# Attention kernel on one core: two buffers for the summed exponentials, narrower columns of maxima, and a rearranged set-up

## The reference, cut to what matters

```python
x = x + proj(softmax(q k^T / sqrt(128)) v)            # q, k, v from group_norm(x): layer 0, one head
t = tokens(x)                                         # 1024 x 128
n = layer_norm(t)
sq, sk = n @ wq_s, n @ wk_s                           # 8 search heads of 16
retrieved = softmax(sq sk^T / 4) @ (n @ wv_r)         # 2 retrievers of 16
gate = softmax over the 2 retrievers of (n @ wq_r) . (retrieved @ wk_ret)
t = t + (gate * retrieved summed over retrievers) @ w_out
w_lora = NF4_TABLE[qidx].reshape(-1, 16) * scales[:, None]   # 128 x 128 codes of 4 bits
t = t + (layer_norm(t) @ w_lora^T) @ W^T
```

## Time and profile before

| what | us |
|---|---|
| median of 3 runs | 5034.42 (5031.06 to 5035.82) |
| the profiled execution | 5030.68 |
| its span | 5028.7 |
| PE busy in it | 4704.0 (94%) |
| POOL busy | 4250.0 (85%) |
| DVE busy | 3893.6 (77%) |
| ACT busy | 3302.2 (66%) |

### The profile page before, as it was taken

How to read it: one execution, slowest core, us unless ns; L and a number is a source line. 1 busy time by engine, 2 the same in 40 slices (tenths; PEclk the granted TensorE clock), 3 DMA queues, 4 the chain that set the end, 5 groups by cost and what they waited for, 6 DMA issues and landing times.

```text
span 5028.7 us, 102045 instructions
## 1 busy us (share of the span) xinstructions
PE 4704.0 (94%) x29838; PEld 2548.5 (51%) x29838; DVE 3893.6 (77%) x8176; ACT 3302.2 (66%) x6657; POOL 4250.0 (85%) x1173
## 2 busy tenths in 40 slices
PE   4899999999999999999999999999999999999986
PEld 3455555555555555555555455555455555555532
DVE  3688887888878888887778887878887878877763
ACT  2466766666766666766676766666767666766654
POOL 1388888888888988888988888988888988888887
PEclk9899999999999999999999999999999999999987
DMA  0111011111011111011111111111111111111010
GB/s 15 38 43 43 31 47 31 39 47 47 26 47 30 39 47 47 30 43 31 39 47 47 34 39 33 37 47 47 38 36 37 32 47 47 43 30 42 28 39 13
DMA packets 92739, 191.77 MB, mean 38 GB/s; under 512 B 16744, under 2 KB 50920, under 8 KB 92400
## 3 DMA queue, kind: packets, MB, share of 16 engines
q1 hardware_dynamic: 92400, 186.45, 12.8%
HBM read 17.53 MB, written 16.78 MB: 7 GB/s over the span
## 4 chain that ended last, share of the span: by engine, by line
issue 38%; PE 34%; POOL 17%; ACT 5%; DVE 5%; POOLq 0%; DMA 0%; ACTq 0%; DVEq 0%; SPq 0%
POOL p_sum L639 16%; PE ps_u L798 7%; PE ps_bank L785 5%; PE ps_bank L749 4%; PE ps_bank L673 4%; PE ps_bank L763 4%; ACT p L956 3%; DVE max_part L1061 2%; PE ps_bank L704 2%; PE ps_bank L807 2%; PE ps_bank L693 1%; PE ps_bank L684 1%; PE ps_bank L815 1%; PE ps_bank L735 1%; ACT h L884 1%
## 5 line engine op out<-in xcount | busy, mean ns | idle before, releaser
L639 POOL TENSOR_TENSOR p_sum<-p_sum,p 128x2048 f32<-128x2048 f32 x768 | 3505.5, 4564 | 266.9 <-ACT p L956 208.5
L1061 DVE TENSOR_REDUCE max_part<-ps_bank 128x1 f32<-128x512 f32 x4096 | 2551.8, 682 | 697.6 <-PE ps_bank L763 693.3
L956 ACT ACTIVATE p<-ps_bank 128x512 f32<-128x512 f32 x4096 | 2154.2, 606 | 704.2 <-PE ps_bank L785 690.9
L798 PE MATMUL ps_u<-p,rv 128*32 128x512 f32 x8192 | 1003.3, 608 | 2.7 <-ACT p L956 2.7
L785 PE MATMUL ps_bank<-q_stack,k_stack 64*128 64x512 f32 x4096 | 888.2, 461 | 105.9 <-ACT p L956 65.8
L639 POOL TENSOR_TENSOR p_sum<-p 128x2048 f32<-128x2048 f32 x128 | 584.1, 4563 | 375.4 <-ACT den_sb L967 205.0
L763 PE MATMUL ps_bank<-k_stack,q_stack 63*128 63x512 f32 x4096 | 828.8, 451 | 55.3 <-ACT p L956 21.7
L785 PEld LDWEIGHTS ps_bank<-q_stack,k_stack 64*128 64x128 f32 x4096 | 370.6, 185 | 665.4 <-ACT p L956 253.9
L763 PEld LDWEIGHTS ps_bank<-k_stack,q_stack 63*128 63x128 f32 x4096 | 363.4, 185 | 523.4 <-ACT p L956 160.5
L749 PE MATMUL ps_bank<-v,p 128*128 128x129 f32 x4096 | 508.6, 279 | 8.2 <-ACT p L956 6.7
L749 PEld LDWEIGHTS ps_bank<-v,p 128*128 128x128 f32 x4096 | 473.2, 191 | 61.1 <-ACT p L956 27.3
(11 more groups left out here) (140 smaller groups left out, 4438.6 us busy)
## 6 DMA issues: line engine op xcount, KB each, us to landing
k_stack<-k_hi SPq DMA_DIRECT2D x256, 128.0 KB, 2.6
q_stack<-q_hi SPq DMA_DIRECT2D x256, 128.0 KB, 2.8
x_sb<-in_x SPq DMA_DIRECT2D x32, 512.0 KB, 3.5
k_stack<-k_lo SPq DMA_DIRECT2D x128, 128.0 KB, 2.6
q_stack<-q_lo SPq DMA_DIRECT2D x128, 128.0 KB, 2.8
t_held<-t_front SPq DMA_DIRECT2D x32, 512.0 KB, 2.9
rqk<-tok_next SPq DMA_DIRECT2D x32, 512.0 KB, 3.6
t_core<-t_held SPq DMA_DIRECT2D x32, 512.0 KB, 3.0
```

Of the source, the lines that this page charges most:

```text
L639: pool.tensor_tensor(p_sum[:, :, :], before, p1[:, step % ring, :, :], ALU.add)\
L798: last = pe.matmul(ps_u[n * QUAD:(n + 1) * QUAD, :], rv[:, key_tile, :], p1[:, step % ring, n, :], start=(key_tile == 0), stop=(key_tile = ...
L956: act.activation(p1[:, step % ring, n, :], bank_of("scores", index // 2, n % 2), ACT.Exp, scale=scale1)\
L1061: dve.tensor_reduce(max_part1[:, phase % 2, i, n, half:half + 1], bank_of("max1", index // 2, side), AXIS.X, ALU.max)\
```

## The change

Four things change; the orders of the engines in the loop stay as they are.

1. `p_sum` gets two buffers, used in turn by phase. The first addition of a phase no longer waits for ACT's copy of the denominators of the phase before, but for TensorE's `den` of the phase before that one (`filled["den"]`), which read the same buffer.
2. The columns of maxima become narrow: `max_cols0` has 8 + 128 columns in place of 1024, `max_cols1` 16 + 128 in place of 512. The tiles that TensorE transposes now overlap; rows of the transposes beyond those used hold other maxima in place of zeros.
3. The 4-bit weight is decoded by DVE: a conversion, 15 independent comparisons into 15 tiles (the code whose value is zero is left out), one reduction over them and one multiplication with the scales. The codes and scales are the first two loads and have a semaphore of their own. The clearing of `k_stack`, `q_stack` and `max_row0` goes to POOL.
4. SP issues the `wk_ret` loads ahead of the rows of ones, and the first image's `x` is loaded between them, in the set-up; `load` returns at once for image 0.

```diff
-        p_sum = sb("p_sum", [P, GROUP, HALF])
+        p_sum = sb("p_sum", [P, 2, GROUP, HALF])
...
-        max_cols0 = sb("max_cols0", [P, tiles, P])
+        max_cols0 = sb("max_cols0", [P, tiles + P])
...
-        max_cols1 = sb("max_cols1", [P, tiles_per_half, P])
+        max_cols1 = sb("max_cols1", [P, tiles_per_half * GROUP + P])
...
+                sp.dma_start(q_index, qidx).then_inc(codes_loaded, 16)
+                sp.dma_start(block_scale[:, :], scales.rearrange("(o k) -> o k", o=P)).then_inc(codes_loaded, 16)
                 loads = [
...
+                sp.wait_ge(blocks_zeroed, 1)
+                for h in range(HEADS):
+                    rows = slice(h * HEAD_DIM, (h + 1) * HEAD_DIM)
+                    sp.dma_start(wk_ret_blocks[rows, rows], wk_ret).then_inc(weights_loaded, 16)
+                sp.dma_start(x_sb[:, :], x_dram[0:1, :, :].rearrange("b c n -> (b c) n")).then_inc(x_loaded, 16)
                 sp.wait_ge(stacks_cleared, 1)
                 for pair in range(PAIRS):
                     sp.dma_start(k_stack[ROWS - 1:2 * ROWS:ROWS, pair, :].bitcast(F32), out_sb[0:2, :])\
                       .then_inc(ones_rows_ready, 16)
...
-                pool.wait_ge(weights_loaded, 16 * (14 + HEADS))
-                link(pool.tensor_copy(q_value, q_index))
-                link(pool.memset(lora, 0.0))
-                for n, value in enumerate(NF4):
-                    link(pool.tensor_scalar(lora_part, q_value, float(n), float(value),
-                                            ALU.is_equal, ALU.mult))
-                    link(pool.tensor_tensor(lora, lora, lora_part, ALU.add))
...
+                pool.memset(out_sb[0:2, :], 1.0)
+                pool.memset(k_stack[:, :, :].bitcast(F32), 0.0).then_inc(stacks_cleared, 1)
+                pool.memset(q_stack[:, :, :].bitcast(F32), 0.0)
+                pool.memset(max_row0[:, :].bitcast(F32), 0.0)
...
+                dve.memset(max_cols0[:, :], 0.0)
+                dve.memset(max_cols1[:, :], 0.0)
+                dve.wait_ge(codes_loaded, 16 * 2)
+                link(dve.tensor_copy(q_value, q_index))
+                levels = [(float(n), value) for n, value in enumerate(NF4) if value]
+                for n, (code, value) in enumerate(levels):
+                    last = dve.tensor_scalar(decoded[:, n, :], q_value, code, value, ALU.is_equal, ALU.mult)
+                link(last)
+                link(dve.tensor_reduce(lora, decoded.rearrange("p n c -> p c n"), AXIS.X, ALU.add))
...
                     if key_tile == 1:
-                        wait(pool, den_evicted, phases * b + phase)
+                        wait(pool, filled["den"], phases * b + phase - 1)
...
-                    before = p1[:, (step - 1) % ring, :, :] if key_tile == 1 else p_sum[:, :, :]
-                    pool.tensor_tensor(p_sum[:, :, :], before, p1[:, step % ring, :, :], ALU.add)\
+                    before = p1[:, (step - 1) % ring, :, :] if key_tile == 1 else p_sum[:, phase % 2, :, :]
+                    pool.tensor_tensor(p_sum[:, phase % 2, :, :], before, p1[:, step % ring, :, :], ALU.add)\
```

More of the change, by code:

```diff
@@ L287, in build @@
         proj_rows, ffn_rows, wq_r_sb, wk_ret_blocks = (setup_tiles[:, n, :] for n in range(3, 7))
-        bias_v, proj_bias, q_value, lora, lora_part = (setup_tiles[:, n, :] for n in range(7, 12))
+        bias_v, proj_bias, q_value, lora = (setup_tiles[:, n, :] for n in range(7, 11))
         q_index = setup_tiles[:, 12, :].bitcast(I32)
         turned = setup_tiles[:, 13:17, :]
+        decoded = setup_tiles[:, 17:17 + len(NF4) - 1, :]
         qk_w = sb("qk_w", [P, 2, P])
@@ L363, in build @@
         weights_loaded = sem("weights_loaded")
+        codes_loaded = sem("codes_loaded")
+        x_loaded = sem("x_loaded")
         blocks_zeroed = sem("blocks_zeroed")
@@ L371, in build @@
         weights_ready = sem("weights_ready")
+        codes_decoded = sem("codes_decoded")
         stacks_cleared = sem("stacks_cleared")
@@ L382, in _ @@
                     (wq_sb[:, :], wq_s), (wk_sb[:, :], wk_s), (wv_r_sb[:, :], wv_r),
-                    (w_out_sb[:, :], w_out), (q_index, qidx),
-                    (block_scale[:, :], scales.rearrange("(o k) -> o k", o=P)),
+                    (w_out_sb[:, :], w_out),
                     (norm_cols[:, 0:1], norm_w.rearrange("(c a) -> c a", a=1)),
@@ L397, in _ @@
                       .then_inc(ones_rows_ready, 16)
[L398 to L401, removed]
             @block.gpsimd
@@ L469, in link @@
                     dve.wait_ge(links.sem, links.next())
[L471 to L476, removed]
+                dve.memset(max_cols0[:, :], 0.0)
[7 more added lines that the diff above has]
+                link(dve.tensor_reduce(lora, decoded.rearrange("p n c -> p c n"), AXIS.X, ALU.add))
+                dve.tensor_tensor(lora.rearrange("p (k j) -> p k j", j=NF4_BLOCK),
+                                  lora.rearrange("p (k j) -> p k j", j=NF4_BLOCK),
+                                  block_scale[:, :].unsqueeze(2).broadcast_to([P, P // NF4_BLOCK, NF4_BLOCK]),
+                                  ALU.mult).then_inc(codes_decoded, 1)
                 dve.wait_ge(pool_ready, 1)
                 dve.tensor_copy(first_row[:, :], ident[:, 0:1].broadcast_to([P, P]))
-                dve.wait_ge(weights_loaded, 16 * (14 + HEADS))
-                dve.tensor_scalar(bias_v, ones[:, :], qkv_bias[:, 2:3], None, ALU.mult)
+                dve.wait_ge(weights_loaded, 16 * (12 + HEADS))
+                dve.tensor_scalar(bias_v, ones[:, 0:1].broadcast_to([P, P]), qkv_bias[:, 2:3], None, ALU.mult)
                 dve.tensor_copy(token_w[:, P:P + HEAD_DIM], wv_r_sb[:, HEAD_DIM:])
@@ L557, in load @@
                 def load(b, index):
+                    if isinstance(b, int) and b == 0:
+                        return
                     wait(sp, h_ready, number_of(b))
@@ L722, in max_rows0 @@
                         last = pe.transpose(out[:, i * P:(i + 1) * P],
-                                            max_cols0[:, half * tiles_per_half + i, :], ident[:, :])
+                                            max_cols0[:, half * tiles_per_half + i:half * tiles_per_half + i + P], ident[:, :])
                     last.then_inc(filled["max_rows0"], 1)
@@ L770, in max_rows1 @@
                     for i in range(tiles_per_half):
-                        last = pe.transpose(out[:, i * P:(i + 1) * P], max_cols1[:, i, :], ident[:, :])
+                        last = pe.transpose(out[:, i * P:(i + 1) * P], max_cols1[:, GROUP * i:GROUP * i + P], ident[:, :])
                     last.then_inc(filled["max_rows1"], 1)
@@ L806, in den @@
                     for n in range(GROUP):
-                        last = pe.matmul(out[n * QUAD:(n + 1) * QUAD, :], ones[:, 0:QUAD], p_sum[:, n, :],
+                        last = pe.matmul(out[n * QUAD:(n + 1) * QUAD, :], ones[:, 0:QUAD], p_sum[:, phase % 2, n, :],
                                          start=True, stop=True)
```

16 lines of the change are left out of this document (6 added, 10 removed).

## The result

The changed kernel takes a median of 4996.4 us (4992.8 to 5000.75, 4 runs) against 5032.82 (5031.06 to 5035.82, 4 runs) of the kernel before: a ratio of 0.9927, 95% interval 0.991 to 0.9945. It is faster by 36 us. The forecast was a gain of 67 us, 4967 us, and a range up to 4993, which the median misses by 3 us.

What follows compares the result with a forecast made beforehand. TensorE (96% busy) and POOL (88%) were taken to bound the loop, a pure chain the set-up. Gains of 26.5 + 26.1 + 12.5 + 2.2 = 67.3 us from 5030.7 gave 4963.4, with 3.7 added 4967 us; range 4943 to 4993.

Steps and rivals of the forecast that it cites:

- Slower, through the clock: Rival for the loop: denser TensorE work gets less clock; 5079 us if 5% ran at the lower level; chance 0.03.
- The set-up, 26.5 us forecast: Before the loop: earlier loads and DVE decoding start the first image's statistics earlier, gaining 26.5 us.
- The hold-up between DVE and POOL: Set-up: DVE's comparisons wait for POOL's memsets, so turned weights are copied at about 18.9, a cost of 4.0 us.
- the alternative: Rival for the set-up: no hold-up, decoding hidden behind the loads, set-up gain 30.5 us, time 4963 us; chance 0.17.
- the terms listed: Set-up after POOL's memsets end at 12.1: comparisons 2.1 us, reduction 2.6, scales 0.3, small work 0.7.
- The loop, 38.6 us forecast: Loop: two buffers let POOL add earlier, removing TensorE's waits at `den` and for `h`, 1.25 us per turn.
- the waits at `den`: TensorE's waits for POOL at `den` vanish except the longest, in the last image: 26.1 us; 0.64 in the turn shown.
- The path to `h`: Loop: POOL reaches `norm_rstd` earlier, so TensorE's wait for `h` vanishes except the first image's: 12.5 us.
- The case in which the whole POOL gap is gained: Rival for the loop: POOL's additions decide the turn, which loses 3.6 us and not 1.25; 4894 us; chance 0.06.
- The one in which the loop gains nothing: Rival for the loop: TensorE's waits return at ACT's or DVE's banks, or ACT is late; 5006 us; chance 0.11.
- The pause ahead of `add.26`: Sign in POOL's additions: exponentials should be ready 0.1 us before `add.26`; a pause there would show the prediction wrong.
- The last image, 2.2 us forecast: End of the run: POOL's last phase no longer waits for the denominators, gaining 2.2 us.

Runs made afterwards that it cites:

- e9: The changed kernel with POOL's clearing of `k_stack` and `q_stack` moved from the set-up into image 0, rows of ones following there: 4989.52 us, ratio 0.9916.
- e5: The changed kernel with POOL's four long set-up memsets waiting until DVE has decoded the weight: 5001.35 us, ratio 0.9938.
- e11: The changed kernel with only an image's last phase starting its additions early, the others waiting for ACT's copy again: 5001.74 us, ratio 0.9937.
- e1: The changed kernel with the old wait for ACT's copy of the denominators; two buffers and new set-up stay: 5005.52 us, ratio 0.9945.
- e2: The kernel before plus two buffers, new wait, narrow columns and a smaller `ones`, with the old set-up: 5020.82 us, ratio 0.9975.
- e3: The changed kernel with `scores.42` to `scores.44` computed twice, in the stretch ahead of the clock's fall: 4977.5 us, ratio 0.9887.
- e4: The changed kernel with score tiles 58, 60 and 61 computed twice, away from the stretch ahead of the fall: 5005.2 us, ratio 0.9946.
- e6: The changed kernel with only score tile 43 computed twice: 4993.28 us, ratio 0.9918.
- e7: The changed kernel with score tiles 43 and 44 computed twice: 4965.59 us, ratio 0.9865.
- e12: The kernel before with score tiles 43 and 44 computed twice, as a control: 5038.13 us, ratio 1.001.

## Why the prediction was wrong, point by point

**The step that failed** is the rival "Slower, through the clock", with its sentence "TensorE's busy share would rise by less than a point, so I give it little". The clock was treated there as a share of the whole loop, and nothing of it came into the sum or the upper end of the range. It acted at one place of the turn, for 3.4 us, and took back 36 us net, about half the gain. It never made the kernel slower, so the rival had the right mechanism at a size and a sign that no case covered. The price was there to be read: the kernel before has a fall of 1.5 us in 3 of 29 turns, which the windows of all turns show and that of a single good one, at 1.00, does not. How many turns would have it could not be read there, but a range up to 29 x 1.5 = 44 us above the forecast would have followed.

**The set-up, 26.5 us forecast, 26.4 measured.** The hold-up between DVE and POOL was as forecast: one comparison stood for 8735 ns beside 0.99 + 3.50 + 3.50 + 0.94 = 8.93 us of POOL memsets, the turned weights were copied at 18.33 + 0.68 = 19.0 (18.9 forecast), and e9 measured the alternative as 4.0 us. The Trainium skill, page SBUF — State Buffer, section Who interferes with whom, states that exclusion, and the runs agree with it, down to a copy of 16 columns held for 5.53 us in e5. The page speaks of the time of one instruction; here the comparison stood until four of POOL's were over. That the total is right to 0.1 us is in part luck, since terms were off and cancelled. The comparisons were over at 13.86 and not 14.2, at about 0.14 us each and not 0.16 (2.12 / 15). The reduction over 1920 elements took 3.37 and not 2.6; it reads its input with a stride, and from SBUF where the row it was priced by reads PSUM; neither was tested as the reason. What stood behind it took less than allowed: the terms listed end at 17.8, so 18.9 has 1.1 more for the two copies (0.42 and 0.68), and small work and copies together took 1.4 (17.58 to 19.01), not 1.8.

**The loop, 38.6 us forecast, some 44 gained before the clock.** Both waits went from the loop, as the rows said. Over the span the waits at `den` shrank by 21.4 us (37.2 to 15.8) and not by 26.1, because waits of 0.78 and 6.18 us came in the last turns, behind the 29. `den.3` was right (0.65 a turn, e11). The path to `h` was probably under-sized: with the other early starts it gave 0.8 a turn, where TensorE's wait was 0.42. The forecast took TensorE's wait at `k0` as all that the delay cost; why the turn gained more stays open. The case in which the whole POOL gap is gained (4894) was far off. The one in which the loop gains nothing (5006) comes nearer to the measured 4996.4 than the forecast does, but for another reason: TensorE's waits did not come back elsewhere, the clock took the gain.

**The pause ahead of `add.26`** was named as a sign that the prediction is wrong, since step 26 had 0.1 us to spare. It came, 1.93 us in the turn shown, and cost nothing, because `add.31` still ends 3 us ahead of `den.3`. So this sign said nothing about the time.

**The last image, 2.2 us forecast, 2.9 measured**; the wait shrank by 2.26 (11.09 to 8.83).

**Narrow columns** were priced at nothing. e1 has them with the old wait, and its turn is 150.0 us as before, so in the loop they cost and gave nothing that the turn shows.

**What stays open.** What e1 to e4, e6, e7 and e12 show is that the falls come with the earlier start of POOL, sit at this stretch, and go when it is filled. They don't show why one turn has a fall and the next, with the same rows ahead of it, has none. The order of the falls has a pattern. Where a turn with a fall takes 150.2 us, falls follow one another: a turn with one is followed by another in 20 of 23 cases in the changed kernel, 23 of 25 in e2, 26 of 27 in e5, 20 of 22 in e6 and 8 of 13 in e9, and falls that follow at this place start 150.2 us apart. Where it takes 150.9 to 151.5 they don't: in none of 2 cases in the kernel before, none of 13 in e4, 2 of 14 in e11. So it may be the length of the turn, and not how tight it is, that brought a fall in nearly every turn. This is argued and not shown. No run tests it, for example with a turn of the changed kernel made a few tenths of a us longer by a wait elsewhere. Nor did a run try another order of the stages, which might give e7's gain without the extra matmuls.

## What to carry to other kernels

Read the granted clock turn by turn, not as a mean, before an edit that changes the length of TensorE's turn: a few turns with a fall in the kernel before show what one costs, and their number can change from 3 to 24 of 29 though the rows ahead of them stay. When falls come behind the same stretch of short, waiting matmuls, try repeated work in that stretch: here four matmuls in an image gave back 31 us. And memsets that moved to GpSimd "for free" held VectorE's comparisons and copies here for as long as they followed each other; moving them in time helped only where nothing of VectorE's stood in the new place.

## What the runs showed of the hardware that was not expected

- The clock fell to the lower level for 3.4 us at a time, up to once in a turn, though TensorE had been busy for 2.91 of the 3.50 us ahead of `values` (after, 2513.93 to 2517.43) and had no gap over 0.32 us there; then it was at 1.00 again. 16 matmuls took 3.61 us in the fall instead of 1.92.
- In four kernels (changed, e2, e5, e6) the falls came turn after turn, 150.2 us from start to start, and in two others (e4, e11), where a turn with a fall takes 151 us, mostly in every second turn.
- More matmuls made the kernel faster: 0.9927 became 0.9865 with two pairs of scores computed twice in an image (e7), and 0.9946 with three pairs at other places (e4).
- The first DVE comparison stood from 3.30 to 12.03, until four POOL memsets were over, and was not let in between them, and a DVE copy of 128 x 16 elements took 5.53 us beside them (e5), with memsets that only write.
- Of one and the same kernel (e9) six executions lay 28.7 us apart, in the order of their mean clock.
